# Attention layers of a decoder: VectorE adds the projected tile and takes its statistics first in the next step, ahead of the newest scores

## The reference

```python
x = x + _L0_attn_ref(_layernorm(x, axis=-1), ...)
x = x + _L0_xattn_ref(_layernorm(x, axis=-1), ctx_1024, ctx_1024, ...)
x = x + _L0_ffn_ref(_layernorm(x, axis=-1), ...)
...
```

```python
q = (x @ Wq).reshape(b, s, h, hd).transpose(0, 2, 1, 3)
k = (x @ Wk).reshape(b, s, h, hd).transpose(0, 2, 1, 3)
v = (x @ Wv).reshape(b, s, h, hd).transpose(0, 2, 1, 3)
scores = jnp.einsum('bhqd,bhkd->bhqk', q, k) * a_k
scores = jnp.where(causal, -jnp.inf, scores)
attn = jax.nn.softmax(scores / np.sqrt(hd), axis=-1)
ctx = jnp.einsum('bhqk,bhkd->bhqd', attn, v)
ctx = ctx.transpose(0, 2, 1, 3).reshape(b, s, h * hd)
return ctx @ Wo + bo
```

## Time and profile before

| | us |
|---|---|
| median of 3 runs | 1791.98 |
| lowest and highest | 1784.16, 1795.23 |
| the profiled execution | 1798.92 |
| its span | 1797.1 |

### The profile page before, as it was taken

How to read it: one execution, slowest core, us unless ns; L and a number is a source line. 1 busy time by engine, 2 the same in 40 slices (tenths; PEclk the granted TensorE clock), 3 DMA queues, 4 the chain that set the end, 5 groups by cost and what they waited for, 6 DMA issues and landing times. The chain is left out here.

```text
span 1797.1 us, 35666 instructions
## 1 busy us (share of the span) xinstructions
PE 1206.6 (67%) x14040; PEld 918.3 (51%) x14040; DVE 1063.3 (59%) x2911; ACT 626.0 (35%) x1479; POOL 665.7 (37%) x729
## 2 busy tenths in 40 slices
PE   7882438827888679374667444199839857666888
PEld 5652437726766646362345343088715616253556
DVE  4879611156999758615776657234379854444773
ACT  2541113306666646023553111022124334333443
POOL 3337444423555445532223114623343331413320
PEclk9885569969999889585877655599978765656788
DMA  9900046440000094040000010345310000000000
GB/s 256 132 2 2 29 118 179 143 130 2 3 2 3 3 136 58 17 120 3 1 1 16 9 24 7 102 139 179 120 35 2 1 1 2 1 1 1 1 2 24
DMA packets 74059, 90.19 MB, mean 50 GB/s; under 512 B 5823, under 2 KB 61186, under 8 KB 73248
## 3 DMA queue, kind: packets, MB, share of 16 engines
q1 hardware_dynamic: 67872, 77.94, 18.6%
q0 software_dynamic: 6016, 9.93, 1.6%
HBM read 57.60 MB, written 32.69 MB: 50 GB/s over the span
## 5 line engine op out<-in xcount | busy, mean ns | idle before, releaser
L846 POOL TENSOR_TENSOR arena<-arena,small 128x1024 f32<-128x1024 f32 x96 | 184.4, 1926 | 154.4 <-ACT arena L704 90.7
L394 POOL TENSOR_SCALAR var_eps<-moments 128x1 f32<-128x1 f32 (+1 forms) x136 | 33.6, 247 | 405.9 <-DVE moments L387 405.9
L606 PE MATMUL ps<-arena,q 64*64 64x512 f32 x768 | 129.9, 751 | 57.8 <-issue 20.6
L755 ACT ACTIVATE arena<-arena 128x1024 f32<-128x1024 f32 x92 | 97.3, 1058 | 179.1 <-DVE arena L920 127.9
L616 PEld LDWEIGHTS ps<-small,arena 128*128 128x128 f32 x736 | 101.8, 167 | 82.6 <-ACT arena L755 48.0
L616 PE MATMUL ps<-small,arena 128*128 128x128 f32 x736 | 124.0, 323 | 24.3 <-ACT arena L755 22.7
L628 PE MATMUL ps<-vx,arena 128*64 128x18 f32 x3072 | 126.6, 228 | 3.7 <-issue 3.0
L628 PEld LDWEIGHTS ps<-vx,arena 128*64 128x64 f32 x3072 | 116.5, 160 | 24.3 <-issue 20.4
L795 ACT COPY arena<-ps 128x512 f32<-128x512 f32 x192 | 104.6, 586 | 53.3 <-PE ps L616 52.3
L1857 POOL TENSOR_TENSOR arena<-arena 128x512 f32<-128x512 f32 x64 | 79.8, 1282 | 104.2 <-DVE arena L1875 104.2
L396 POOL TENSOR_TENSOR rstd<-var_eps,minus_half 128x1 f32<-128x1 f32 (+1 forms) x136 | 105.3, 774 | 11.3
(11 more groups left out here) (324 smaller groups left out, 2786.0 us busy)
## 6 DMA issues: line engine op xcount, KB each, us to landing
expert_ring<-L2f_in SPq DMA_DIRECT2D x23, 704.0 KB, 4.2
expert_ring<-L0f_in SPq DMA_DIRECT2D x23, 578.0 KB
slots_L0f<-blank SPq DMA_DIRECT2D x1, 8385.0 KB, 56.9
slots_L2f<-blank SPq DMA_DIRECT2D x1, 8385.0 KB, 56.8
small<-small_in SPq DMA_DIRECT2D x1, 4231.5 KB, 19.2
expert_ring<-L1f_in SPq DMA_DIRECT2D x8, 512.0 KB
arena<-slots_L0f SPq DMA_DIRECT2D x23, 129.0 KB, 3.1
arena<-slots_L2f SPq DMA_DIRECT2D x23, 129.0 KB, 3.6
```

The costliest lines, as they stand in the source:

```text
L606: last = pe.matmul(c.ps[part(b), m], c.q[part(m), at:at + S], kx(t)[part(m), b * 512:(b + 1) * 512], start=True, stop=True)
L755: act.activation(buf(k), buf(k), ACT.Relu if sparse else ACT.Exp, scale=exp_scale).then_inc(s.probs_ready, 1)
L846: g.tensor_tensor(kx(t).rearrange("p (b h k) -> p b h k", b=2, k=S), bcast(of_tile, 2, HEADS // 2), bcast(bcast(c.w("head_of_row"), 2, S), ...
```

## The change

In VectorE's loop, `add` and `measure` of a tile go from the end of a step to the start of the next one, and `scale` goes to the step after the one in which it stood. The loop has one step more.

```diff
-            for k in range(nt + lag + 3):
+            for k in range(nt + lag + 4):
                 ahead, step = k // HT + 1, k % HT
+                if 0 <= k - lag - 3 < nt:
+                    add(k - lag - 3)
+                    if not rms:
+                        v.wait_ge(s.y_added, k - lag - 2)
+                        measure(v, following, c.x, k - lag - 3)
                 if k < nt:
                     if sparse:
                         less_threshold(k)
@@ -959,13 +964,8 @@
                         shift(k)
                 if 0 <= k - lag - 1 < nt:
                     normalise(k - lag - 1)
-                if 0 <= k - lag - 2 < nt:
-                    add(k - lag - 2)
-                    if not rms:
-                        v.wait_ge(s.y_added, k - lag - 1)
-                        measure(v, following, c.x, k - lag - 2)
-                if not rms and 0 <= k - lag - 3 < nt:
-                    scale(v, following, c.x, c.h, k - lag - 3)
+                if not rms and 0 <= k - lag - 4 < nt:
+                    scale(v, following, c.x, c.h, k - lag - 4)
                 if latent and ahead < quarters:
                     if step in (1, 2):
                         for t in range(HT * ahead + 2 * step - 2, HT * ahead + 2 * step):
```

## The result

The changed kernel is slower. In the same set of runs it took 1799.61 us in the median (11 runs, 1789.90 to 1811.63), the kernel before 1793.25 (11 runs). The ratio is 1.005, 95% interval 1.0025 to 1.0074. The medians differ by 6.4 us, the ratio stands for 9, and its interval for 4 to 13. The forecast was 1790.6 with small gains and losses that cancel. Executions more than 1.5% above the fastest of their kernel stay out of all ratios; the only profiled execution of `only_latent`, a kernel that comes further down, is one of them (4828 us). The profiled execution of the changed kernel took 1797.71 us (span 1795.9) and that of before 1798.92 (1797.1): single executions scatter by some 8 us either way, so two spans say nothing here and the reading goes by steps and layers.

A forecast was written before the change was run, and what follows sets the result against it. No engine is full, so the wait ending last in each step bounds the kernel. Terms 1.5 + 0.5 - 2.3 + 0.5 - 1.4 - 0.2 = -1.4 us, put on the median 1791.98, gave 1790.6 us; range 1781 to 1801.

The forecast's parts named there:

- What moves: In VectorE's loop, add (A) and statistics pass behind scaling (S) and extra work; a layer's last three tiles keep order.
- First layer: First attention layer, with bias: L920 overlaps GpSimd's spreading longer and takes about 1.49 us; +1.5 us, bounds 0 and 3.4.
- Plain layer: Layer with plain scores: later statistics lengthen the loop through GpSimd, two steps take 8.09 us; +0.5 us.
- Latent layer: Next quarter's normalisation starts 0.73 us earlier, the step ahead wins 0.4: -2.3 us; overlap in last tiles: +0.5 us.
- the cover: Latent layer: delayed add and statistics run while other engines make the new quarter's keys and scores, keeping the 0.73 us.
- Sparse layer: Both sparse halves: scaling goes into the wait for the projection, -0.23 us in each of six steps; -1.4 us.
- Decay and causal layers: Decay layer: VectorE is full, 0; causal layer: extra work once on the path behind an add, -0.2 us.
- the loop in every layer: Rival: later statistics cost through GpSimd in all 64 steps that spread keys, 14.7 us; 1805 us, chance 0.12.
- The rival that held: TensorE's granted clock falls once or twice more, 5 us per stretch; 1801 us, chance 0.08.

The follow-up runs named there:

- only_latent: The new order in the latent layer alone, against the kernel before; not told apart from no change, its only profiled execution took 4828 us.
- the added matmuls: Two more matmuls with unused results in each sparse-layer step, put into both the kernel before and the changed kernel; new order against old, both with them: 0.9974 and 0.9970.
- busy pair: The kernel before and the changed kernel, each with two unused matmuls more per sparse-layer step; new order against old 0.9974, repeated 0.9970.
- after: The changed kernel itself, against the kernel before: 1799.61 us, ratio 1.005.
- bias_psum: The changed kernel with the first layer's biased scores left in PSUM: 1799.61 us, 1.0046 against the kernel before.
- keys_free: The changed kernel with GpSimd working on the deviation of a tile one older: 1793.33 us, 1.0010 against the kernel before.
- tails_only: The changed kernel with an unused matmul ahead of each projection in the last steps of the latent and decay layers: 1801.39 us, 1.0040 against the kernel before.
- only_bias: The new order in the first attention layer alone, against the kernel before; its time was not told apart from no change.
- all_again: The changed kernel as it is, timed again in another set: 1.0014 against the kernel before.

## Why the prediction was wrong

- *What moves*: right in the loop, wrong at its end. "At the end of a layer the last three tiles keep their order" does not hold: S passes A there, and L628 waits for A. It cost 0.2 us in L1x (the last three tiles take 7.17 instead of 6.97 us) and 0.2 in the one step of L2a that has the high clock in both.
- *First layer*: 1.49 was forecast for L920, 1.51 measured, and the wait goes with PSUM. The layer's mean is +0.5, since a low stretch of the clock comes and goes in it in kernels of both orders; where the clock stays at 1.00 it is +1.5, as forecast. By the Trainium skill, "SBUF — State Buffer", section "Who interferes with whom", the shared ports are an exclusive lock and the loser blocks for all of the other instruction; the estimate by that rule is 1.22 + 0.43 = 1.65. The trace has 1.51, and the measurement decides.
- *Plain layer*: two steps of 8.09 forecast, 8.12 measured. The term was 0.5 and the layer lost 0.9. The pairs of steps that were counted give their 0.5. One more step is in the loop (to N6, 4.14 instead of 3.93 to 3.96), 0.2, and the last three tiles are the other 0.2.
- *Latent layer*: L873 was to start 0.73 us earlier and did so by 0.71; the step ahead of it was to win 0.4 and won 0.51. In the second quarter the failed step is the cover: "if that cover were gone, the 0.73 would come back" looked at VectorE's A and M. What took 0.55 of it back was TensorE's clock, in the last matmuls of the same step. Yet in three of six traces the forecast's terms came out whole up to N12, -2.2 and +0.5. The step that failed in all six is the end: the last three tiles were priced at nothing and lost 2.1 to 3.0 us, nearly all of it through the clock. Together +2.1 instead of -1.8: the largest miss, and the surest.
- *Sparse layer*: 0.23 us in a step forecast, 0.26 measured, with and without the added matmuls. The sum was given "apart from the clock". Nearly every one of its steps is at the low clock, and a rise near the end of a half is worth 0.6 to 3.7 us (27.97 without it, 24.2 to 27.4 with it), against 0.8 that three steps gain. +1.6 instead of -1.4.
- *Decay and causal layers*: the decay steps are 6.39 instead of 6.38, as forecast. The last three tiles of the layer took 7.65 in five of seven traces of the old order and in two of eight of the new one, and 10.1 to 11.9 in the others, so its +1.5 stays open. In the causal layer the step from N3 to N4 takes 11.58 instead of 11.78, or 11.37 instead of 11.57 where L452 is hit (the last section): the forecast -0.2. The rest of its spread is that hit and the clock, in both orders.
- *Rivals*: the loop in every layer did not happen; only L1x shows it. The rival that held is that of the clock, 1801 us at a chance of 0.08. It was given so little because "it can as well go the other way". That treats the clock as luck. At the end of the latent layer it is not: 6.97 to 6.98 in seven traces of one order, 9.1 or 10.0 in six of the other. The change put a bias on it. The mechanism was named, and the failed step is its price: nothing in the sum, on the ground that gains and losses by the clock are alike. In the traces the latent layer comes out 3.9 us above its term and the sparse layer 3.0. That the measured time, 1799.6, lies close to that rival's 1801 is partly luck: it priced two stretches of 5 us, and the runs have several smaller losses. The prediction had rows at the low clock in three layers and asked of none of them what a shift of 0.2 to 0.7 us would do.

What stays open: why the rise in the sparse layer and the fall in the latent one come where they do, and the share of L3a and L3f in the time that was lost. The busy pair's gain of 5 us is about what the sparse layer shows in the traces (65.7 us in the mean of two traces against 71.0, N0 to N7 of both halves); then the other layers would have lost nothing, where the table above has 6 us, 4.5 of them sure (L0a, L1x, L2a). The timings are not fine enough to say which.

## What to carry to other kernels

Ahead of a reordering that is worth tenths of a microsecond in a step, mark where TensorE's granted clock is low and where it changes, and ask whether TensorE is on the path there: a rise that does not move with the work gives back what was won ahead of it. Where TensorE goes through a whole loop at the low clock and is on the path, unused matmuls can be worth more than the reordering: in the sparse layer they brought the new order to 0.4 to 0.5% under before, and the old order to nothing that can be told from before. In the last tiles of a layer they cost. Follow the new order through the last steps of the loop too, where the wide instructions that covered a wait are gone. And compare layers over many traces of both orders, like clock with like: here one pair of spans had the wrong sign.

## What had not been expected of the hardware

In the causal layer, L452 (inputs from SBUF, 128x128, four times) is hit hard by a spreading that runs beside it. In the changed kernel:

```profile
1663.35 1.91 POOL L846 TENSOR_TENSOR arena<-arena,small 128x1024 f32<-128x1024 f32 x1 [1.75 <-PE ps L606]
...
1663.80 2.39 DVE L452 SCALAR_TENSOR_TENSOR hn<-h,rstd,small 128x128 f32<-128x128 f32 x4
```

In the kernel before, with no spreading beside it:

```profile
1668.70 1.13 DVE L452 SCALAR_TENSOR_TENSOR hn<-h,rstd,small 128x128 f32<-128x128 f32 x4
```

They are together from 1663.80 to 1665.26, 1.46 us, and the four take 1.26 more, which is again the time together less some 0.2. A second group of four took 2.78. The 17 traces part clearly by it. In five of them both groups are hit, and it takes 79.3 to 81.7 us; in the other twelve both take 1.13, and it takes 74.0 to 76.9. Four of the five have the new order in this layer (`after`, `bias_psum`, `keys_free`, `tails_only`) and one, `only_bias`, the old; `all_again`, the same kernel as `after`, is not hit. So the new order alone does not bring it about. What decides it was not found.
